# A graph network's edge stage: the looped tile's source one-hots move from VectorE to ScalarE

## The reference

```
x = layernorm(x + L0(x, src, dst))                  # segment_sum((x @ Wn)[src], dst) and an image attention
x = layernorm(x + L1(x, edges, edge_type))          # two relation layers, w[r] = sum_b att[r, b] * basis[b]
x = layernorm(x + L2(x, edges))                     # five layers: segment_sum(h[src], dst)
x = layernorm(x + L3(x, edges, edge_weight))        # segment_sum((x @ W)[src] * edge_weight, dst)
```

## Time and profile before

| | us |
|---|---|
| Median of 3 runs | 1828.7 (1823.96 to 1830.86) |
| The profiled execution's own time | 1824.01 |
| Its span in the profile | 1822.2 |
| PE busy in the span | 1759.3 (97%) |
| DVE busy | 859.9 (47%) |
| ACT busy | 580.5 (32%) |
| Granted TensorE clock, mean | 0.999 |

### The profile page before, as it was taken

How to read it: one execution, slowest core, us unless ns; L and a number is a source line. 1 busy time by engine, 2 the same in 40 slices (tenths; PEclk the granted TensorE clock), 3 DMA queues, 4 the chain that set the end, 5 groups by cost and what they waited for, 6 DMA issues and landing times.

```text
span 1822.2 us, 22269 instructions
## 1 busy us (share of the span) xinstructions
PE 1759.3 (97%) x7346; PEld 850.8 (47%) x7346; DVE 859.9 (47%) x1877; ACT 580.5 (32%) x1185; POOL 11.0 (1%) x37
## 2 busy tenths in 40 slices
PE   5989888999999999999999999999999999999998
PEld 3555555533334444444444444444544444444444
DVE  7888886479883221112122225334252433594123
ACT  2555544466774211222110001232323323232000
POOL 1000000000000000000000000000000000000000
PEclk9999999999999999999999999999999999999999
DMA  7999989810302401000011115300000010021111
GB/s 181 267 263 274 256 236 241 310 35 13 132 24 74 164 0 47 0 1 24 0 40 42 35 35 227 159 1 29 1 1 29 1 41 0 1 82 58 35 47 47
DMA packets 46692, 157.27 MB, mean 86 GB/s; under 512 B 8726, under 2 KB 10670, under 8 KB 38006
## 3 DMA queue, kind: packets, MB, share of 16 engines
q1 hardware_dynamic: 44704, 146.43, 26.5%
q10 hardware_dynamic: 1878, 9.44, 1.4%
HBM read 120.19 MB, written 35.65 MB: 86 GB/s over the span
## 4 chain that ended last, share of the span: by engine, by line
PE 83%; DMA 7%; DVE 6%; issue 2%; DVEq 1%; ACT 1%; POOL 0%; POOLq 0%
PE psum L1541 31%; PE psum L1527 31%; PE psum L1782 7%; DMA hs<-in_L_gnn_basis 4%; PE psum L1455 2%; PE psum L1422 2%; PE psum L1732 2%; DMA adj<-in_L_gnn_basis 2%; PE psum L1629 2%; PE psum L1616 1%; PE psum L1454 1%; PE psum L1493 1%; PE psum L1708 1%; DVE hs L710 1%; DMA wb<-in_L_gnn_Wf 1%
## 5 line engine op out<-in xcount | busy, mean ns | idle before, releaser
L1541 PE MATMUL psum<-hs,adj 128*128 128x512 f16 x2880 | 636.2, 379 | 0.0
L1527 PE MATMUL psum<-wb,xt 128*128 128x512 f32 x1056 | 458.1, 593 | 0.8 <-DVE hs L1011 0.8
L1541 PEld LDWEIGHTS psum<-hs,adj 128*128 128x128 f16 x2880 | 281.2, 98 | 330.7 <-issue 11.0
L1527 PEld LDWEIGHTS psum<-wb,xt 128*128 128x128 f32 x1056 | 198.6, 190 | 245.9 <-issue 244.2
L1292 ACT ACTIVATE ua<-ua 128x512 f32<-128x512 f32 x60 | 37.7, 629 | 314.9 <-DVE ua L1088 181.1
L1084 DVE SCALAR_TENSOR_TENSOR vt<-psum,scl,xt 128x512 f32<-128x512 f32 x60 | 44.8, 746 | 192.7 <-PE psum L1541 192.7
L1019 DVE TENSOR_TENSOR vt<-psum,adj 128x512 f32<-128x512 f32 x24 | 16.6, 692 | 249.3 <-PE psum L1527 249.3
L1527 PE MATMUL psum<-adj,xt 128*128 128x512 f32 x288 | 130.1, 594 | 0.0
L1782 PE MATMUL psum<-hs,adj 128*128 128x512 f32 (+1 forms) x312 | 123.8, 559 | 0.0
L1455 PE MATMUL psum<-hs 128*128 128x192 f32 x404 | 99.7, 329 | 0.0
L1280 ACT ACTIVATE lnst<-lnst,bcol 128x1 f32<-128x1 f32 x24 | 7.1, 295 | 280.1 <-DVE lnst L988 270.5
(11 more groups left out here) (253 smaller groups left out, 1715.7 us busy)
## 6 DMA issues: line engine op xcount, KB each, us to landing
hs<-in_L_gnn_basis SPq DMA_DIRECT2D x38, 960.0 KB, 11.4
adj<-in_L_gnn_basis SPq DMA_DIRECT2D x26, 960.0 KB, 12.9
aw_scratch<-xt ACTq DMA_DIRECT2D x12, 768.0 KB, 10.0
adj<-aw_scratch SPq DMA_DIRECT2D x1, 9216.0 KB, 36.5
x_scratch<-adj SPq DMA_DIRECT2D x24, 256.0 KB, 2.4
hs<-x_scratch SPq DMA_DIRECT2D x24, 256.0 KB, 2.6
ts_scratch<-adj SPq DMA_DIRECT2D x2, 2304.0 KB, 17.8
as_scratch<-adj SPq DMA_DIRECT2D x1, 4608.0 KB, 16.7
```

The costliest lines, as they stand in the source:

```text
L1527: x = pe.matmul(psum[:, bank, :], xt[:, i, k, :], w[:, k, :], start=first and k == 0, stop=last and k == 3)
L1541: x = pe.matmul(psum[:, i % 2 + (4 * half if own else 0), :], adj[:, m, j, P * i:P * i + P], hs[:, t, half, j, :], start=n == 1 or (own an ...
```

## The change

The `onehot_s` part of the looped tiles is no longer made by VectorE but by ScalarE, with two activations: the absolute difference between a row of numbers 0 to 127 and the edge's source, then relu(1 - that), which is 1 where they are equal and 0 elsewhere. The intermediate goes through a new buffer, `apart`, and ScalarE waits on its own semaphore between the two. In ScalarE's order these run in a loop of their own, `sources`, for window w + 1, ahead of the eviction of window w. ScalarE now loads and unpacks the packed word instead of a single number. TensorE has one more wait for each looped tile.

```
+        apart_t = sb("apart", [P, P], F32)
+        apart = apart_t[:, :]
...
+        apart_ready, source_ready = sem("apart_ready"), sem("source_ready")
...
-            def source(k, t):
-
-                dve.tensor_scalar(onehot_s[k], iota_s[:, 0:P], ecol[:, 0, bass.ds(t, 1)], None, ALU.is_equal)
-
...
                     last = nc.s_assert_within(first + q + 2, 0, EC - 1, skip_runtime_bounds_check_because=why)
-                    source(LOOPED, last)
                     keys(LOOPED, last, n, u)
...
-            following = act.value_load(wrow_i[0:1, 2, 0:1], min_val=1, max_val=NW * MOST)
+            def window(w):
+                return act.value_load(wrow_i[0:1, 0, w:w + 1], min_val=0, max_val=PACKED)
+
+            def sources(first, steps, before):
+
+                with act.Fori(0, steps) as q:
+                    t = nc.s_assert_within(first + q + 2, 0, EC - 1, skip_runtime_bounds_check_because="a tile of this stretch")
+                    act.wait_ge(onehot_free[LOOPED], before + q + 1)
+                    act.activation(apart, iota_s[:, 0:P], ACT.Abs, bias=ecol[:, 0, bass.ds(t, 1)], scale=-1.0).then_inc(apart_ready, 1)
+                    act.wait_ge(apart_ready, before + q + 1)
+                    act.activation(onehot_s[LOOPED], apart, ACT.Relu, bias=1.0, scale=-1.0).then_inc(source_ready, 1)
+
+            act.wait_ge(c_ready, 7)
+            first, steps, before = unpack(window(0))
+            sources(first, steps, before)
             for w in range(NW):
                 s, u, b = w // PER, w % PER, w % RING
-                through = following
+                through = before + steps
                 if w + 1 < NW:
-                    following = act.value_load(wrow_i[0:1, 2, w + 1:w + 2], min_val=1, max_val=NW * MOST)
+                    first, steps, before = unpack(window(w + 1))
+                    sources(first, steps, before)
                 if u == 0 and s >= 2:
...
                     pe.wait_ge(onehot_ready[LOOPED], before + q + 1)
+                    pe.wait_ge(source_ready, before + q + 1)
                     counts(b, LOOPED, False)
```

## The result

The changed kernel takes 1838.59 us (median of 5 runs, 1837.33 to 1843.51) against 1828.61 us before (5 runs, 1823.96 to 1830.86). The ratio is 1.0062, with a 95% interval of 1.0047 to 1.0078: slower by 10 to 11 us. The profiled execution took 1838.59 us and has a span of 1836.7 us, 14.5 us more than the profiled one before, which lay near the lowest of its runs; so absolute differences between the two traces are some 4 us too large.

A forecast was written before the change was run, and what follows sets the result against it. It took PE (89% busy), DVE (83%) and DMA as together near their limit in the 292 us edge stage. Terms -5 - 0 + 5 + 1.3 = +1.3 us on 1828.7 gave 1830 us, range 1819 to 1846.

The forecast's parts named there:

- the forecast case: Whole kernel: the summed terms hold, 1830 us, with its own range of 1824 to 1837; chance 0.37.
- slower by over 0.5%: Whole kernel: outcome above 1837.8 us, from late copies, table loads and the top of the forecast; chance 0.23.
- the rival of late copies: ScalarE reaches the eviction over about 1.0 us behind PE's end; turn lots stall: +15 to +29, 1844 to 1858; chance 0.2.
- three signs of being wrong: On ScalarE: register work adds to each eviction, source later than 1 us, or a table load in the loop.
- The relief: Edge stage: VectorE loses its 106 source instructions, taking 5 us off the chain, with ends 0 and 8.
- The second looped tile: In ten windows with two looped tiles, PE's 1.03 us stall for the slot's refill stays: 0 to -1 us, taken as 0.
- The source in ordinary windows: Source ready some 0.95 us behind PE's end, while PE first runs two static tiles of 0.49 us: not late, 0.
- The copies: Turn-lot copies behind ScalarE's sources stall PE in windows without basis lots: +5 us; +1.3 where the next window has two looped tiles.
- What DMA hides: From 136 to 196 and 252 to 314 us, transfers set the chain, so these 122 us can hardly gain or lose.
- The table load in each loop: ScalarE loads a table in each loop's body and again behind it: 202 loads, +190, 2019 us; chance 0.03.

The follow-up runs named there:

- run 5: The changed kernel, but VectorE keeps its 106 source instructions, writing a buffer that nobody reads: 1840.43 us, ratio 1.0057.
- run 2: The changed kernel with ScalarE's order turned: eviction of window w first, then the sources of w + 1, then the side lots' copies: 1830.49 us, ratio 1.0001.
- run 3: The changed kernel, but VectorE makes the sources again and ScalarE's loop writes an unused buffer that TensorE doesn't wait for: 1837.6 us, ratio 1.0032.
- Run 6: The kernel before with each chunk of relation weights loaded by half, the matmuls reading that half twice: 1823.55 us, ratio 0.9959.
- runs 7 and 8: Both load weight chunks by half. 7: kernel before without VectorE's source (zeros instead), 1814.28 us, ratio 0.9915. 8: changed kernel, 1838.31 us, ratio 1.0043.
- run 1: The changed kernel with the absolute difference made ahead of ScalarE's wait for TensorE's release of the slot: 1828.45 us, ratio 0.9989.
- run 11: The changed kernel with the absolute difference ahead of the wait and two source buffers used by windows in turn, with a computed wait value: 1840.53 us, ratio 1.0055.

## Why the prediction was right, and where it wasn't

The time, 1838.6 us, lies in the stated range of 1819 to 1846, but 9 us above the forecast of 1830 and above the forecast case's own range, which ended at 1837. It is "slower by over 0.5%", which had a chance of 0.23. The range held it only because it took in a lower part of the rival of late copies. The sum had +1.3 us; 10 were measured. Of its signs, the stage's end at 314 us give or take 5 didn't come (329.3), and two of its three signs of being wrong did: the source is ready later than 1 us behind PE's end (1.03 us below), and register work adds 0.12 us to each eviction. Step by step:

**The relief (-5 us).** Alone it is -3.5 us, and PE's waits for DVE fall by 8.5 us; both fit. Beside ScalarE's new work no worth can be measured (run 5 and the changed kernel, 1.0057 and 1.0062). I added it to a sum in which another term held PE in its place. VectorE was relieved and then waited 43.9 us for PE.

**The second looped tile (0).** The step said that the stall stays. It grew. The timeline of the changed kernel around one, against the earlier trace rows:

```profile
122.62 0.49 PE L1468 MATMUL psum<-hs 128*128 128x192 f32 x2
...
123.40 0.40 ACT L1174 ACTIVATE apart<-hs 128x128 f32<-128x128 f16 x1 [1.82 <-PE psum L1468]
123.52 0.37 DVE L709 TENSOR_SCALAR hs<-hs 128x192 f32<-128x192 f16 x1
123.83 0.31 ACT L1176 ACTIVATE hs<-apart 128x128 f32<-128x128 f32 x1
...
124.28 0.32 PE L1467 MATMUL psum<-hs 128*128 128x384 f16 x1 [1.17 <-ACT hs L1176]
```

PE ends at 122.62 + 0.49 = 123.11. The absolute difference starts 0.29 us later, not 0.17; the relu ends at 124.14, and PE goes on at 124.28, 0.14 later. VectorE's keys are ready at 123.89, so VectorE is no longer what holds PE. The stall is 1.17 instead of 1.03 us. The activations were sized right; what was missed is 0.12 us of register operations ahead and 0.14 us of hand-over behind, around every second looped tile.

**The source in ordinary windows (0).** Here the prediction failed as put: "In an ordinary window the source isn't late either". It compared 0.95 us with two static tiles, 0.98 us, a margin of nothing. PE waited for the source 21 times, 19.6 us in all, of which ten second tiles make 11.7 us; the other 11 waits, up to 1.4 us each, follow absolute differences that start 0.5 to 2.2 us behind the release instead of 0.29, because ScalarE came late to begin with. But this wait stands where VectorE's stood: PE's waits for one-hots of either engine are 27.3 us before and 26.5 after. And run 2 keeps 18.8 us of it at a ratio of 1.0001. So it explains why the relief was lost, and little of the slowdown.

**The copies (+5 + 1.3).** This was the right mechanism, and the term of the sum that was too small: ScalarE's load alone costs +5.9 us by ratio, and up to the whole loss by time (run 3). PE waits 14.7 us for turn copies at 22 places, some 12 us of it where no basis lot stands between two turn lots, as the prediction had it, against the 5 + 1.3 us that it counted. One window and the next in the changed kernel:

```profile
115.21 0.40 ACT L1174 ACTIVATE apart<-hs 128x128 f32<-128x128 f16 x1 [0.45 <-PE psum L1468]
...
115.64 0.31 ACT L1176 ACTIVATE hs<-apart 128x128 f32<-128x128 f32 x1
...
116.07 0.49 ACT L1191 ACTIVATE wb<-psum 128x384 f16<-128x384 f32 x1
...
116.33 0.49 PE L1468 MATMUL psum<-hs 128*128 128x192 f32 x2
...
116.67 0.60 ACT L1154 ACTIVATE xt<-psum 128x512 f32<-128x512 f32 x1
...
117.19 0.40 ACT L1174 ACTIVATE apart<-hs 128x128 f32<-128x128 f16 x1
...
117.32 0.66 PE L1447 MATMUL psum<-ident,xt 128*128 128x128 f32 x4 [0.50 <-ACT xt L1154]
```

In the first the absolute difference starts at 115.21 and the copy at 116.67, 1.46 us later: 0.40 + 0.03 + 0.31, then 0.12 to the eviction at 116.07, then the eviction's 0.60. In the next one, PE ends its looped tile at 116.33 + 0.49 = 116.82, finds ScalarE still in the turn copy until 117.27, and starts its turn lot at 117.32, 0.50 us late. Over the stage the eviction starts 1.24 us behind PE's end (median from the timeline; 0.03 before), where I had taken 0.95. Run 2, with the loop behind the eviction, has the copy 0.5 us earlier. Its trace shows why. The eviction starts 0.04 us behind PE's end (median), where the absolute difference needed 0.29; in one window it starts at 117.70 us, the loop's register operations run beside it from 117.75 to 118.18, and the absolute difference follows at 118.30 without a gap. The 0.12 us between relu and eviction don't stand ahead of the copy either. No run changed these operations alone.

**What DMA hides.** The prediction read from the chain that "122 of 292 us can neither gain nor, within limits, lose", since transfers carry 81% and 72% of it there. The chain by line of the changed kernel from 136 to 196 us, against the second of the earlier trace rows, has no transfer among its largest lines:

```profile
by line: PE psum L1468 16.9%; PE psum L1435 14.9%; PE psum L1467 10.8%; issue 9.9%; ACT apart L1174 6.6%; PE psum L1447 4.7%; ACT adj L1148 4.6%; ACT wb L1191 4.5%; ACT xt L1154 3.8%; PE psum L1444 3.7%; ACTq L1167 3.3%; ACTq L1171 2.9%; AC
```

A chain names what came last, if only by a hair. The slack was in another view: PE's whole wait for chunks is 8 us. Run 6 confirms that: without these waits the kernel before gains 7.5 us. In runs 7 and 8 the relief's step is -8 us instead of -3.5 and the change's +15 instead of +10 or 11, which fits, but neither growth is clear of the noise, and a part of run 7's is clock.

**What the prediction had no term for** is the clock: 2.9 us more of busy PE in the changed kernel's profile, behind stalls of PE that the change lengthened or added.

**The rivals.** That ScalarE's copies become the wait, "when ACT reaches the eviction later than about 1.0 us behind PE's end", is what came true by its condition (1.24 us), at a price nearer the forecast than its own +15 to +29; with half loads it is +15. The table load in each loop didn't happen. The Trainium skill's page "ScalarE: Activation LUTs", section "Table sets: the hidden batching unit", has relu, copy and absolute value in every set. The trace agrees as far as it goes: one load of 1283 ns in the stage, for a loop that holds two of them between copies.

**In sum.** PE's idle time in the stage by what ended it, from the waits of each profile from 22 to 330 us (the copies are those of turn and basis lots):

| | one-hots from VectorE | source from ScalarE | ScalarE's copies | chunks | ratio |
|---|---|---|---|---|---|
| before | 27.3 | | 0.5 | 8.1 | 1 |
| changed | 6.9 | 19.6 | 14.7 | 4.3 | 1.0062 |
| run 1 | 16.3 | 3.0 | 5.7 | 11.3 | 0.9989 |
| run 2 | 6.6 | 18.8 | 7.1 | 7.1 | 1.0001 |
| run 3 | 26.8 | | 13.9 | 2.4 | 1.0032 |
| run 5 | 13.0 | 18.2 | 12.5 | 3.6 | 1.0057 |

The change swaps VectorE's late one-hots for ScalarE's late source, about one for one. What is new are 14.2 us of waits for late copies, of which fewer waits for chunks give back 3.8, and 2.9 us of lower clock. The three kernels with 12 us and more of waits for copies (changed, 3 and 5) are the slow ones, the two with half of that (1 and 2) are level with before, whether the source is late (run 2) or not (run 1). The forecast had named these copies and counted 6.3 us for them, set 5 us of relief against them that the late source took back, and left out the clock.

## What to carry to other kernels

Work moved to an engine that is half idle is free only if the engine isn't needed at that moment: ScalarE here was idle until TensorE's release and wanted by three parties right behind it, so the part of the work that needs no release belongs ahead of it (run 1), or what others wait for goes first (run 2). Register arithmetic and a computed wait value take time as instructions do, and on an engine that is late they lie open (0.12 us a loop here, 0.4 us with the computed value of run 11). Gains of one engine and costs of another must not be summed where both hold the same third engine; and how much a transfer can absorb is read from who waits for it, not from its share of the chain.

## What the runs showed of the hardware

A wait whose value is a register expression held ScalarE for 0.43 us (median of 106 in run 11, none below 0.28) between two dependent activations, with five sequencer operations in the gap, where simple values held it for 0.03 us.

The granted clock fell from 1.00 to half twice in the changed kernel's stage, each time when PE had stood idle twice in short order for over 1 us; matmuls with `onehot_t` took 0.52 instead of 0.33 us there. A third such pair of stalls brought no fall, and before, whose stalls of 1.03 us stand alone, kept 1.00 in the stage of its profile. No run was made to look at the clock by itself.

The kernel before is spread over 16 us from run to run of the same code (24 runs), and over 4.1 us with half loads (1820.86 to 1824.97, 12 runs). That fits transfers whose rate differs from run to run and that PE feels only where they are near the limit. The clock doesn't order those 24 runs (the slowest, 1837.98 us, has a mean of 0.999, the one with the lowest, 0.994, took 1832.8). No run looked at it by itself, and the numbers of runs differ.
